# Moving the reads of the tiles' owners into the products ahead, and the first sorted loads past a wait

## What is computed

```python
xn = layernorm(x)
s = linear_attention(xn, W)            # q, k = elu(.)+1; V = (q KV) / (q k_sum)
g = silu(ffn(xn))                      # each row goes to ONE of 8 experts: argmax of its gate logits
x = x + s * g
xn = layernorm(x)
s = block_attention(xn, W_qkv, W_out, b_out)       # causal, blocks of 128 rows
g = silu(ffn1(xn, ...))
x = x + s * g
# the first layer's ffn, for the expert e of a row:
#   inter = relu(xn @ wg[e])**2 * (xn @ wu[e]);  out = inter @ wd[e]
```

## Time and profile before

| | |
|---|---|
| three timed runs | 513.07, 515.52, 516.12 us; median 515.52 |
| the profiled execution's own time | 513.82 us |
| its span | 511.1 us |
| busy in the span: PE, DVE, ACT, POOL | 97%, 88%, 77%, 62% |
| granted TensorE clock, mean | 0.996 of 2.4 GHz |
| instructions | 12177 |

### The profile page before, as it was taken

How to read it: one execution, slowest core, us unless ns; L and a number is a source line. 1 busy time by engine, 2 the same in 40 slices (tenths; PEclk the granted TensorE clock), 3 DMA queues, 4 the chain that set the end, 5 groups by cost and what they waited for, 6 DMA issues and landing times.

```text
span 511.1 us, 12177 instructions
## 1 busy us (share of the span) xinstructions
PE 497.0 (97%) x3567; PEld 465.0 (91%) x3567; DVE 452.2 (88%) x1426; ACT 392.0 (77%) x894; POOL 315.9 (62%) x370
## 2 busy tenths in 40 slices
PE   6999999999999999999999999999999999999996
PEld 5999999999999999789999988897888889888885
DVE  6799999999999988949989948999999999999985
ACT  4778878787878784467878855887888888888885
POOL 4468876767676877452222028899988887775200
PEclk9899999999999999999999999999999999999999
DMA  8933322222222115447878663266657656665311
GB/s 223 251 114 95 107 91 87 89 85 83 84 84 84 43 52 165 151 132 230 256 239 255 217 200 116 75 131 153 141 130 151 134 141 130 138 141 111 78 46 62
DMA packets 59302, 67.68 MB, mean 132 GB/s; under 512 B 11880, under 2 KB 53616, under 8 KB 59248
## 3 DMA queue, kind: packets, MB, share of 16 engines
q1 hardware_dynamic: 44304, 38.69, 24.8%
q0 software_dynamic: 14944, 28.32, 23.0%
HBM read 39.85 MB, written 27.13 MB: 131 GB/s over the span
## 4 chain that ended last, share of the span: by engine, by line
PE 87%; DVE 6%; POOL 2%; issue 2%; ACT 1%; DMA 1%; SPq 0%; DVEq 0%
PE v_ps L1495 9%; PE q_ps L1473 9%; PE gu_ps L1143 6%; PE s_ps L1515 5%; PE y_ps L1162 3%; PE k_ps L168 3%; PE m_ps L168 3%; PE t_ps L1119 3%; PE m_ps L170 3%; PE m_ps L169 3%; PE k_ps L169 3%; PE k_ps L170 3%; PE tq_ps L168 3%; PE tq_ps L169 3%; PE tq_ps L170 3%; PE tq_ps L400 3%
## 5 line engine op out<-in xcount | busy, mean ns | idle before, releaser
L1920 POOL DMA_INDIRECT four<-expert_rows,gather_u x64 | 75.0, 1172 | 36.7 <-DMA expert_rows<-y 17.9
L957 POOL DMA_INDIRECT sorted_rows<-xn,row_u x64 | 67.6, 1057 | 17.2 <-issue 14.4
L946 POOL TENSOR_TENSOR xn<-xn 128x512 fp32r<-128x512 f32 x32 | 43.2, 1350 | 31.1 <-ACT xn L563 30.9
L1473 PE MATMUL q_ps<-xt,wqk 128*128 128x256 f32 x256 | 60.5, 379 | 0.0
L1495 PE MATMUL v_ps<-wvo,xt 128*128 128x256 f32 x248 | 58.7, 379 | 0.0
L1473 PEld LDWEIGHTS q_ps<-xt,wqk 128*128 128x128 f32 x256 | 48.5, 190 | 6.9 <-issue 0.4
L209 POOL DMA_DIRECT2D four<-sorted_rows x36 | 19.9, 553 | 52.1 <-issue 40.3
L1495 PEld LDWEIGHTS v_ps<-wvo,xt 128*128 128x128 f32 x248 | 44.8, 190 | 4.8
L1935 POOL TENSOR_TENSOR rstd<-var_eps,neg_half 128x4 f32<-128x4 f32 x32 | 35.6, 1114 | 12.4 <-DVE var_eps L1758 12.3
L1926 POOL DMA_DIRECT2D res<-in_L_attn_x x26 | 35.0, 1366 | 9.8 <-DVE res L1722 8.2
L168 PE MATMUL tq_ps<-xt,wq 128*128 128x256 f32 x128 | 38.4, 300 | 1.9 <-DVE xt L697 1.9
(11 more groups left out here) (280 smaller groups left out, 1759.4 us busy)
## 6 DMA issues: line engine op xcount, KB each, us to landing
expert_rows<-y SPq DMA_DIRECT2D x35, 256.0 KB, 3.1
four<-in_L_attn_x SPq DMA_DIRECT2D x32, 256.0 KB, 2.8
out_rows<-att SPq DMA_DIRECT2D x31, 256.0 KB, 2.2
res<-in_L_attn_x POOLq DMA_DIRECT2D x26, 256.0 KB, 4.7
four<-sorted_rows POOLq DMA_DIRECT2D x36, 128.0 KB, 2.8
four<-sorted_rows SPq DMA_DIRECT2D x36, 128.0 KB, 2.4
wdn<-in_L_ffn_wd SPq DMA_DIRECT2D x2, 512.0 KB, 7.9
sorted_rows<-res SPq DMA_DIRECT2D x8, 128.0 KB, 6.4
```

The source lines that it names most:

```text
L946: nc.gpsimd.tensor_tensor(xn2[:, s, 1], xn[:, i], xn2[:, s, 0].bitcast(F32), ALU.subtract).then_inc(g["xn_split"], 1)
L957: nc.gpsimd.indirect_dma_start(out=z.sorted_dram.ap(), out_offset=bass.IndirectOffsetOnAxis(ap=row_u[:, i // CU, k:k + 1], axis=0), in_=xn ...
L1473: m = nc.tensor.matmul(q_ps[:, j, :], wqk[:, k, j * P:(j + 1) * P], xt[:, i % 2, k, :], start=(j == 0 and k == 0), stop=(k == KD - 1), ski ...
L1920: nc.gpsimd.indirect_dma_start(out=moe[:, n % SLOTS, t, :], out_offset=None, in_=z.expert_dram.ap()[0:(z.SLOTS - 1) * P, :], in_offset=bas ...
```

## The change

Three edits. No instruction is added or removed.

1. The six reads ahead of the first turn are spread over the values of START[1], START[2] and START[3]: two to each unit, one behind the first product of each of its two tiles, so that three products of the unit follow the first read and one the second. The wait for `tables_made` 2 moves with them, to behind START[0].
2. In steps 14, 17 and 20 the read moves from the end of the step (behind turn(m+3)) to behind gate_up(m), ahead of turn_hidden(m-1) and down(m-2).
3. SyncE's `load_sorted` moves ahead of its wait for `kv_ready`.

```diff
-def whole_values(nc, pe, z, p, banks, free):
+def whole_values(nc, pe, z, p, banks, free, between=None):
...
             m = nc.tensor.matmul(banks[:, t, 0:z.NV], parked(z, v)[:, j, t * P:(t + 1) * P], z.kvf[:, slot, j, :], start=(j == 0), stop=(j == z.KD - 1))
+            if between and j == 0:
+                between(t)
...
             sp.dma_start(w2_end[:], W_qkv[D - 1, :].partition_broadcast(P)).then_inc(g["weights_loaded"], 16)
+            z.load_sorted(sp, 0)
             sp.wait_ge(z.first_sems["kv_ready"], len(SPLIT_ROWS) + len(WHOLE_ROWS))
-            z.load_sorted(sp, 0)
...
                     gate_up(m, m % QUAD, experts_of(m), m >= 2)
+                if m in OWNER_LOADS:
+                    load_owners(OWNER_LOADS[m])
...
-                if m in OWNER_LOADS:
-                    load_owners(OWNER_LOADS[m])
...
-            for p, before in zip(START[:4], (*TAIL, START[0]), strict=True):
-                values(p, before)
+            def values(p, before, owners_from=None):
+
+                load = owners_from is not None and (lambda t: load_owners(owners_from + t * OCTET))
+                whole_values(nc, pe, z, p, value_banks[p], before + 1, load)
+
+            values(START[0], TAIL[0])
             pe.wait_ge(z.first_sems["tables_made"], 2)
-            for first in range(0, OWNERS, OCTET):
-                load_owners(first)
+            values(START[1], TAIL[1], 0)
+            values(START[2], TAIL[2], 2 * OCTET)
+            values(START[3], START[0], 4 * OCTET)
```

More of the change, by code:

```diff
@@ L1198, in step @@
                     turn(m + 3, (m + 3) % QUAD, True)
-                if m in OWNER_LOADS:
-                    load_owners(OWNER_LOADS[m])
                 for f in WEIGHT_TURNS.get(m, ()):
                     turn_weight(f)
-            def values(p, before):
-                whole_values(nc, pe, z, p, value_banks[p], before + 1)
-            for p, before in zip(START[:4], (*TAIL, START[0]), strict=True):
-                values(p, before)
+            def values(p, before, owners_from=None):
+                load = owners_from is not None and (lambda t: load_owners(owners_from + t * OCTET))
+                whole_values(nc, pe, z, p, value_banks[p], before + 1, load)
+            values(START[0], TAIL[0])
             pe.wait_ge(z.first_sems["tables_made"], 2)
-            for first in range(0, OWNERS, OCTET):
-                load_owners(first)
+            values(START[1], TAIL[1], 0)
+            values(START[2], TAIL[2], 2 * OCTET)
+            values(START[3], START[0], 4 * OCTET)
             for i in range(2):
```

## The result

| | before | after |
|---|---|---|
| timed runs (19 of each, in turns) | median 514.22 us (512.48 to 516.12) | median 512.53 us (510.1 to 514.38) |
| ratio to before, 95% interval | | 0.9965 [0.9952, 0.9977] |
| span of the profiled execution | 511.1 us | 510.8 us |
| granted TensorE clock, mean | 0.996 | 1.000 |
| instructions | 12177 | 12177 |

The ratio makes it 1.8 us faster (1.2 to 2.5; the ratio's distance from 1 by 514.2), a gain of a third of a per cent.

What follows compares the result with a forecast made beforehand. PE was taken to bound the kernel, with 87% of the chain that ended last. Entry -1.1, loop -0.9 and SyncE 0 gave -2.0 us, from 514.7 to 512.7 us; own range 511.5 to 513.9, blurred 510.6 to 516.0.

Steps and rivals of the forecast that it cites:

- The mechanism at the entry: Ahead of gate_up(0): PE's 1.89 us idle goes, ScalarE's late copy leaves 1.1 us of gain.
- both its terms: The two predicted gains: 1.1 us at the entry, ahead of gate_up(0), and 0.9 us in the loop.
- the first rival: No read shows before work needing no register: entry 1.2, loop 1.5, together -2.7 us, 512.0 us; chance 0.12.
- PE's issue wait goes, ScalarE's copy is late next: Ahead of the first turn: 1.9 us wait vanishes; about 1.0 us for ScalarE's copy appears before gate_up(0).
- The first read, taken at 0.2, bounds 0.1 to 0.4: In START[1], behind its first product: the read exposes 0.2 us of PE time, 0.1 to 0.4.
- VectorE's lateness: At START[3]: VectorE, busy until 216.31, can't take its sums before 216.23, covering 0.2 us of PE delay.
- 1.1 forecast: At the entry: gate_up(0) starts 1.1 us earlier, bounds 0.5 to 1.2.
- The other five at 0: Remaining reads among the values: hidden behind four matmuls (0.87 us) each, cost 0, at worst 0.1 each.
- The loop, gain 0.9 (old 1.5, new 0.6): Steps 14, 17, 20: three reads cost 0.6 us (0.3 to 0.9) behind gate_up instead of 1.5, gaining 0.9.
- SyncE's move at 0: SyncE's loads before the first turn: issued up to 1.5 us earlier, worth 0, bounds -0.1 to +0.2 us.
- I let it reach the end whole: Behind the loop: PE or the last store sets the pace, so all 2.0 us reach the kernel's end.

Runs made afterwards that it cites:

- e4: Changed kernel with ScalarE copying the first turn ahead of scaling START[3]; ratio 0.9985 to the kernel before.
- e13: Changed kernel with e4's ScalarE order, each value read one product later, loop reads at steps 19, 21, 23; ratio 0.9951 to the kernel before.
- e1: Kernel before with only the first edit, the six reads spread among the values; ratio 0.9993 to the kernel before.
- e8: Changed kernel with each of the six value reads doubled; the doubles were not in the trace, so it repeats the changed kernel; ratio 0.9972 to the kernel before.
- e10: Changed kernel with two of SyncE's four stores of a round moved behind the first two loads of the next; ratio 0.9969 to the kernel before.
- e16: Changed kernel with every fourth store of the expert loop issued by ScalarE instead of SyncE; ratio 1.0015 to the kernel before.
- e12: Changed kernel with all six reads in START[1], three behind the first product of each tile; ratio 1.0034 to the kernel before.
- e2: Kernel before with only the second edit, the reads of steps 14, 17 and 20 behind gate_up; ratio 0.9995 to the kernel before.
- e3: Kernel before with only the third edit, SyncE's sorted loads ahead of its wait; ratio 0.9996 to the kernel before.
- e5: Kernel before with a further read at the end of steps 22 to 33, of which three stayed (31 to 33); ratio 1.0032 to the kernel before.
- e6: Kernel before with a further read behind gate_up of steps 22 to 33, of which three stayed (31 to 33); ratio 1.0046 to the kernel before.
- e17: e13 with e16's store on ScalarE; ratio 0.9999 to the kernel before.

## Why the prediction was right

The predicted 512.7 us met 512.53 (against a before of 514.7 assumed and 514.22 measured), and the gain of 2.0 met 1.8 (1.2 to 2.5). The mechanism at the entry was right; that the sum came out so near is in part luck, since both its terms were taken too high and a loss that it lacked is there as well. The time alone speaks only weakly against the first rival (2.7 us); the product that stood behind a read settles that. Step by step:

- **PE's issue wait goes, ScalarE's copy is late next.** Shown: the two waits in the trace, and e4 and e13, where the order on ScalarE alone takes the second wait from 1.02 to 0.34.
- **The first read, taken at 0.2, bounds 0.1 to 0.4.** Too small: 0.49 in after, 0.41 in e1, 0.55 in e4, 0.34 or 0.35 in e8, e10 and e16, by the starts of the products. In after the read began at 210.5, when the array had already begun START[1] (210.39), and took 774 ns: there was no lead. This is also why VectorE's lateness did not cover it: from START[0], its sums of START[3] come at 7.74 in place of 7.38, and it waits 0.26 for PE. Hence an entry gain of 0.83 in after, 0.98 at most (e10 and e16) and 0.56 in e1, for 1.1 forecast.
- **The other five at 0.** Right: the later groups stand 0.22 apart per matmul in after, e1 and e8. It holds for two reads per eight matmuls; at six it breaks (e12).
- **The loop, gain 0.9 (old 1.5, new 0.6).** The new price was right in after, e2 and e8: 0.74, 0.65, 0.56, and step 14 is the worst of the three in each, as the queue's position had said. In e10 it is 0.91, with step 20 the worst. The old one was read from one execution; in e3 it is 1.1, and e1, e5 and e6 have e3's steps. So the gain is 0.2 to 0.5 by these, up to 0.9 with before's own 1.5, and the forecast took the top of it. And it belongs to those steps: e5 and e6 found hardly a difference at steps 31 to 33, and other steps (19, 21, 23) were no better in e13.
- **SyncE's move at 0.** Its issues came 1.5 us earlier in after (210.89 to the 212.39 of the earlier trace rows) and 0.6 in e3, and nothing waited for them in either kernel. Right as far as it shows; the timing alone allows 1 us either way.
- **"I let it reach the end whole."** That is the step that does not hold. In after's profiled execution the loop gave back 1.7 of 1.97 us to loads, in e1 and e13 up to 1.9 and 2.8 us of VectorE's time went to one store, in e8 next to nothing was lost. Nor is it the mark of the new entry: before, e2 and e3 show no such wait, but e5 and e6, whose entry is the old one, have 1.6 and 1.4 us of VectorE's time in it. I had read DMA's cover only at the border, for the first tiles, and took the loop's 0 waits of before as room, without asking how long SyncE's round is beside PE's. The issue times of before had the answer: 8.1 and 9.2 us.

The terms as the traces have them, 0.6 to 1.0 and 0.2 to 0.9, give 0.8 to 1.9 without losses to transfers. The measured 1.8 (1.2 to 2.5) is near their top, so something may balance what the transfers take. One candidate is a term that the prediction did not have, the clock. Five profiled kernels keep the old wait ahead of the turn (before, e2, e3, e5, e6), and in one of them, e2, the granted clock fell to half right behind it and 1.7 us were lost; in the eight that spread the reads over three units (after, e1, e4, e8, e10, e13, e16, e17) it stayed at 1.00 there. If one execution in five loses 1.7, removing the wait is worth 0.3 us on average. That is an estimate from a single fall and not shown. The timed executions lend it no support: their mean granted clock is 0.9978 over 151 of kernels with the old wait and 0.9980 over 102 of the eight others, which is 0.1 us, known to about 0.3. What the transfers take back on average is open as well: a profile is one execution of each kernel, and the three edits' own timings are too coarse.

## What to carry to other kernels

A read into an engine's registers costs only what the work already handed to the engine does not cover: count the instructions queued ahead of it, and put it where at least four matmuls of 0.22 us stand (e13), not two (after). That is shown ahead of the loop; in the loop the price moved between nothing and 0.6 us with the step and the execution, and no place was shown to be free. Spread such reads; three in a row behind two matmuls cost 1.50 and 0.86 us (e12). Before booking a gain of the bounding engine, measure the round of every queue that feeds it: here SyncE's 8 to 10 us stood beside 8.1 of PE, which no wait of the kernel before gave away, though its issue times did.

## What I had not expected of the hardware

- A read of 8 words took some 590 ns mostly. The first of the six took 774 to 788 in all fourteen traces, before or behind the change, and single reads of the loop took up to 1274.
- A store's issue on SyncE took 0.41 us as a rule and 1.82 once in after; the next loads moved by 1.4, a read of start rows by 0.6 more, and PE stood for 0.85 us at the end of it, 15 us later. It is not rare: from 226 to 296 us the longest issue is 1.11 to 1.86 in after, e1, e4, e5, e6, e10 and e13, and 0.83 at most in the other seven. Those seven with a slow issue are also the ones in which VectorE waits over 1 us for stores; which of the two brings the other is not shown.
- The granted clock fell to half behind a wait of 1.50 in e2, and did not behind 1.89 in the kernel before, nor behind the same wait in e5 and e6, nor behind 1.44 in e3. Behind e12's 1.50 and 0.86, with 0.4 us of work between, it fell too.
- Reads into registers that are written again before use are not in the executed program (e5, e6, e8): doubling such a read measures nothing.
